# Scores and mix of two self attentions cut into eighths on TensorE, with transposes and projections between the pieces, and ScalarE's copies put in the same order

## The reference, cut to what matters

```python
# stage "sa0"
x = x + _L0_attn_ref(_layernorm(x, axis=-1), ...)
q = rms_norm(proj(Wq), qn_w); k = rms_norm(proj(Wk), kn_w); v = proj(Wv)
attn = jax.nn.softmax(jnp.einsum('bhnd,bhmd->bhnm', q, k) * scale, axis=-1)
out = jnp.einsum('bhnm,bhmd->bhnd', attn, v)       # then @ Wo.T
# stage "sa1": heads go through latents of 32, rotary turning and a causal mask
q_lat = q @ q2l_w.T + q2l_b; k_lat = k @ kv2l_w.T + kv2l_b; v_lat = v @ kv2l_w.T + kv2l_b
q_lat = q_lat * cos + _rotate_half(q_lat) * sin     # k_lat likewise
att = jnp.einsum('bhql,bhkl->bhqk', q_lat @ wqk_w.T + wqk_b, k_lat) * L ** (-0.5)
att = softmax(where(causal, att, -inf)); y = (att @ v_lat) @ l2o_w.T + l2o_b   # then @ cproj_w.T + cproj_b
```

## Time and profile before

| what | value |
|---|---|
| three timed runs | 2615.22, 2619.82, 2624.42 us |
| the profiled execution's own time | 2611.48 us |
| its span in the profile | 2609.7 us |
| mean granted TensorE clock | 0.974 |
| TensorE busy | 2437.4 us, 93% |
| VectorE, GpSimd, ScalarE busy | 65%, 57%, 49% |
| sa0, from its first transposes to its last output product | 1247.1 to 1416.2 us |
| sa1, likewise | 2384.7 to 2582.6 us |

### The profile page before, as it was taken

The page is one execution under the profiler, slowest core; times in us unless marked ns, Lnnn a source line. Parts: engine busy times, 40 slices in busy tenths (PEclk is TensorE's granted clock), DMA queues, the critical chain, the costliest instruction groups (busy, mean ns, idle before and its releaser), DMA issues. The chain is left out here.

```text
span 2609.7 us, 64368 instructions
## 1 busy us (share of the span) xinstructions
PE 2437.4 (93%) x24498; PEld 1899.7 (73%) x24513; DVE 1691.6 (65%) x3969; ACT 1282.5 (49%) x2972; POOL 1475.4 (57%) x1669
## 2 busy tenths in 40 slices
PE   6898999999999999998797999599999999999997
PEld 3456787888878878786565678478888888886565
DVE  5677868686868786874475744466656665653665
ACT  3565656565656565654342333244454445443443
POOL 6896767675757676754672245665456445322233
PEclk9999999999999999999997999799999999999999
DMA  5232211121111111110002459532234224210001
GB/s 166 104 146 84 58 38 48 33 50 35 46 38 42 40 45 36 48 28 14 30 5 85 152 177 303 186 119 77 68 96 103 73 68 97 69 47 15 3 4 35
DMA packets 224820, 190.04 MB, mean 73 GB/s; under 512 B 89218, under 2 KB 212675, under 8 KB 224515
## 3 DMA queue, kind: packets, MB, share of 16 engines
q1 hardware_dynamic: 208994, 153.92, 19.8%
q0 software_dynamic: 9216, 27.28, 4.4%
q10 hardware_dynamic: 6304, 4.72, 0.6%
HBM read 151.53 MB, written 34.31 MB: 71 GB/s over the span
## 5 line engine op out<-in xcount | busy, mean ns | idle before, releaser
L289 POOL TENSOR_TENSOR rk<-ss,neg_half 128x32 f32<-128x32 f32 x64 | 348.7, 5448 | 246.5 <-DVE ss L271 246.5
L1771 PE MATMUL banks<-rowsT,qk 128*128 128x257 f32 x1024 | 243.5, 380 | 0.9 <-ACT qk L1692 0.9
L322 ACT ACTIVATE ksq<-kT 128x512 f32<-128x512 f32 x256 | 161.1, 630 | 160.2 <-DVE kT L265 160.2
L265 DVE COPY kT<-banks 128x512 f32<-128x512 f32 x256 | 176.9, 691 | 61.0 <-PE banks L376 56.9
L376 PE MATMUL banks<-x_hi,wk_hi 128*128 128x256 f32 x1024 | 213.5, 289 | 1.1 <-DVE kT L265 1.0
L1771 PEld LDWEIGHTS banks<-rowsT,qk 128*128 128x128 f32 x1024 | 189.5, 190 | 27.9 <-ACT qk L1692 1.2
L376 PE MATMUL banks<-x_hi,wk_lo 128*128 128x256 f32 x1024 | 206.8, 284 | 0.0
L376 PE MATMUL banks<-x_lo,wk_hi 128*128 128x256 f32 x1024 | 205.6, 282 | 0.3 <-DVE x_lo L257 0.3
L1224 ACT ACTIVATE score<-score,ntop 128x289 f32<-128x289 f32 x256 | 135.4, 530 | 115.5 <-DVE ntop L1104 115.4
L1581 POOL DMA_INDIRECT parts<-scratch_expert,address x128 | 133.6, 1044 | 91.3 <-DVE residual L1477 45.6
L1610 POOL CAST r_hi<-diff 128x512 fp32r<-128x512 f32 x64 | 41.5, 649 | 248.4 <-PE banks L1797 247.6
(11 more groups left out here) (358 smaller groups left out, 6520.2 us busy)
## 6 DMA issues: line engine op xcount, KB each, us to landing
rowsT<-in_ctxT SPq DMA_DIRECT2D x64, 257.0 KB, 2.9
wgu<-in_expert_gu SPq DMA_DIRECT2D x64, 256.0 KB, 3.9
rows<-in_ctx SPq DMA_DIRECT2D x64, 256.0 KB, 3.2
raw<-in_ctx SPq DMA_DIRECT2D x61, 256.0 KB, 2.7
scratch_qT<-qT SPq DMA_DIRECT2D x16, 512.0 KB, 2.7
scratch_kT<-kT SPq DMA_DIRECT2D x16, 512.0 KB, 3.0
q<-scratch_qT SPq DMA_DIRECT2D x64, 128.0 KB
kT<-scratch_kT SPq DMA_DIRECT2D x64, 128.0 KB
```

Of the source, the lines that this page charges most:

```text
L265: nc.vector.tensor_copy(m.kT[:, k, 2 * i:2 * i + 2, 0:ROWS], banks[i % 2].rearrange("p (a r) -> p a r", a=2)).then_inc(s.kT, 1)
L289: nc.gpsimd.tensor_tensor(m.rk[:], m.ss[:], kit.neg_half[:, 0:KF * H], ALU.pow).then_inc(s.rk, 1)
L322: nc.scalar.activation(m.ksq[:, 2 * i:2 * i + 2, :], m.kT[:, k, 2 * i:2 * i + 2, 0:ROWS], ACT.Square).then_inc(s.ksq, 1)
L1771: mm = nc.tensor.matmul(score[h][:, c - h * HALF, 0:CTX], m.qk[:, f, j, c * BT:(c + 1) * BT, :].rearrange("p h q -> p (h q)"), m.rowsT[:, ...
```

## The change

On TensorE the 64 products of the scores are issued in eight parts of 8, those of the mix likewise. In a step the parts of the scores are now mixed with the row transposes (after the first part) and with the transposes of queries and keys in four pairs (after parts five to eight). The parts of the mix are mixed with the latent product (sa1, after the second part), the values (after the fourth) and the groups of the projection (after the fifth, in sa1 also the sixth). The last three parts of the mix in sa0, two in sa1, therefore come behind the projection, right ahead of the next scores. The first part of the scores waits for `shift` of the tile before as well. On ScalarE the copy of the keys comes ahead of the exponentials, and the copy of the mix (`mix_T`) behind the values and `inner`. No product, copy or byte is added or removed.

```diff
@@ ScalarE
                 def step(n, has):
                     if has(2):
                         queries_T(n + 2)
+                    if has(2):
+                        keys_T(n + 2)
                     if has(1):
                         exps(n + 1)
-                    if has(2):
-                        keys_T(n + 2)
                     if has(5):
                         rows_T(n + 5)
-                    if has(0):
-                        mix_T(n)
                     if rotary and has(2):
                         latent_T(n + 2)
                     if has(4):
                         values(n + 4)
                         inner(n + 4)
+                    if has(0):
+                        mix_T(n)
...
@@ TensorE
+                def scores(n, eighth):
+                    if eighth == 0:
...
+                        pe.wait_ge(s.qT, n + 1)
+                        pe.wait_ge(s.kT, n + 1)
+
+                        past(pe, s.shift, n)
+                        past(pe, s.yT, n - 1)
...
+                    c = eighth // 2
+                    for b in (eighth % 2 * 2, eighth % 2 * 2 + 1):
...
+                    if eighth == 7:
+                        mm.then_inc(s.s_ps, 1)
...
                 def step(n, has):
-                    if has(1):
-                        scores(n + 1)
-                    if has(2):
-                        queries_keys_T(n + 2, has(3))
-                    if has(5):
-                        rows_T(n + 5)
+                    for e in range(8):
+                        if has(1):
+                            scores(n + 1, e)
+                        if e == 0 and has(5):
+                            rows_T(n + 5)
+                        if e >= 4 and has(2):
+                            queries_keys_T(n + 2, e - 4, has(3))
                     if has(-1):
                         output(n - 1)
-                    if has(0):
-                        mix(n, has(1))
-                    if rotary and has(2):
-                        latent_T(n + 2)
-                    if has(4):
-                        values(n + 4)
-                        project(n + 4)
+                    for e in range(8):
+                        if has(0):
+                            mix(n, e, has(1))
+                        if rotary and e == 1 and has(2):
+                            latent_T(n + 2)
+                        if e == 3 and has(4):
+                            values(n + 4)
+                        if e in (4, 5) and has(4) and e - 4 < QK // 512:
+                            project(n + 4, e - 4)
```

More of the change, by code:

```diff
@@ L2367, in values @@
                     product(kit.psum(1)[:, D:2 * D], n, slice(QK, QK + D), rotary).then_inc(s.v_ps, 1)
[L2369 to L2380, removed]
@@ L2382, in queries_keys_T, with project @@
-                def queries_keys_T(n, more):
-                    pe.wait_ge(s.qk, n + 1)
-                    if more:
+                def project(n, i):
+                    if i == 0:
+                        pe.wait_ge(s.xlT, n + 1)
+                        past(pe, s.qT, n - 1)
+                        past(pe, s.kT, n - 1)
                         if rotary:
-                            pe.wait_ge(s.lat, n * 2 + 4)
-                            pe.wait_ge(s.cosed, n * 2 + 4)
-                        else:
[L2390 to L2394, removed]
+                            past(pe, s.lat, n * 2)
+                            past(pe, s.cosed, n * 2)
+                        else:
+                            past(pe, s.raw, n)
+                    product(kit.psum(2 + i), n, slice(i * 512, (i + 1) * 512), rotary).then_inc(s.qk_ps, 1)
@@ new lines, in queries_keys_T @@
+                def queries_keys_T(n, part, more):
+                    if part == 0:
+                        pe.wait_ge(s.qk, n + 1)
+                        if more:
+                            if rotary:
+                                pe.wait_ge(s.lat, n * 2 + 4)
+                                pe.wait_ge(s.cosed, n * 2 + 4)
+                            else:
+                                pe.wait_ge(s.raw, n + 2)
+                    i = part // 2
+                    for c in (part % 2 * 2, part % 2 * 2 + 1):
+                        mm = nc.tensor.transpose(kit.psum(2 + i)[:, c * P:(c + 1) * P], m.qk[:, n % 2, (i * HC + c) * BT:(i * HC + c + 1) * BT, :].rearrange("p h l -> p (h l)"), kit.ident[:])
+                    if part % 2 == 1:
+                        mm.then_inc((s.qT_ps, s.kT_ps)[i], 1)
@@ L2398, in latent_T @@
                     nc.tensor.matmul(kit.psum(2), wm.wqk[:], r.qrT[:], start=True, stop=True).then_inc(s.qrT_ps, 1)
[L2400 to L2410, removed]
-                        for a in range(BT):
-                            nc.tensor.matmul(kit.all[:, 4 + a, 0:P], kit.ident16[:], r.causal[:].rearrange("p c k -> p (c k)"), start=True, stop=False, skip_group_check=True)
-                    for c in range(HC):
-                        for b in range(BT):
[L2415 to L2433, removed]
+                def scores(n, eighth):
+                    if eighth == 0:
+                        if n == 0 and extra is not None:
+                            pe.wait_ge(extra.w, 1)
+                        pe.wait_ge(s.qT, n + 1)
+                        pe.wait_ge(s.kT, n + 1)
+                        past(pe, s.shift, n)
+                        past(pe, s.yT, n - 1)
+                        if rotary:
+                            if n == 0:
+                                pe.wait_ge(s.masked, 1)
+                            for a in range(BT):
+                                nc.tensor.matmul(kit.all[:, 4 + a, 0:P], kit.ident16[:], r.causal[:].rearrange("p c k -> p (c k)"), start=True, stop=False, skip_group_check=True)
+                    c = eighth // 2
+                    for b in (eighth % 2 * 2, eighth % 2 * 2 + 1):
+                        for a in range(BT):
+                            rows, tokens = slice(a * S, (a + 1) * S), slice(b * S, (b + 1) * S)
+                            mm = nc.tensor.matmul(score[tokens, a, c, :], m.qT[rows, n % 2, c, tokens], m.kT[rows, n % 2, c, tokens],
+                                                  start=not rotary, stop=True, skip_group_check=True)
+                    if eighth == 7:
+                        mm.then_inc(s.s_ps, 1)
@@ new lines, in mix @@
+                def mix(n, eighth, more):
+                    if eighth == 0:
+                        pe.wait_ge(s.pT, n + 1)
+                        if more:
+                            pe.wait_ge(s.shift, n + 2)
+                    f, i = eighth // 4, eighth // 2 % 2
+                    for a in (eighth % 2 * 2, eighth % 2 * 2 + 1):
+                        for b in range(BT):
+                            rows, part, h = slice(b * S, (b + 1) * S), slice(a * S, (a + 1) * S), f * 2 * BT + 2 * a + i
+                            mm = nc.tensor.matmul(mixed[part, b, f, :], m.v[rows, n % VB, h, :], m.pT[rows, n % 2, place(h), :],
+                                                  start=(i == 0), stop=(i == 1), skip_group_check=True)
+                    if eighth == 7:
+                        mm.then_inc(s.y_ps, 1)
```

## The result

Five runs of the changed kernel took 2686.80 to 2702.74 us, median 2691.49, against 2619.94 before: 1.0281 times as long, 95% interval 1.0263 to 1.0299. It is slower, by 71.5 us where I had forecast some 41, and outside the range. The profiled execution took 2686.8 us, its span is 2685.0 us and the mean granted clock 0.966. Its span is 75.3 us longer than before. Busy times have hardly moved, except TensorE's, which also counts time at the lower clock. The profiled execution is the fastest of the five. The others show a mean granted clock from 0.966 down to 0.957 and spans up to 2700.9 us, so differences of some us between two profiles can be the clock's alone.

A forecast was written before the change was run, and what follows sets the result against it. TensorE, 93% busy, was taken as the bound, with stops for instructions mostly in the mix. 9.5 (sa0) + 25.8 (sa1) + 3.6 - 2.4 + 2.4 + 2.7 = 41.6 us gave a forecast of 2660 us, range 2636 to 2686.

The forecast's parts named there:

- the wait for `yT`: Scores (sa0) or mask product (sa1) wait for the mix's late copy: 1.70 and 2.16 us behind the projection's end.
- the shift wait: Mix waits for VectorE's maximum and subtraction of the scores, no longer covered: some 0.4 us a step, both stages.
- the price of a split: TensorE's way to a large product and back: net 0.11 us, bounds 0 and 0.23; 0.05 in sa1's mix.
- the clock: TensorE's granted clock falls to half behind long gaps: two such cases taken, +2.7 us.
- the tails: Three last steps of each stage, without projection, get the later mix: +2.4 us together, bounds 0 and 4.
- Rivals A: Even instruction stream wins as copies hide behind half-idle ScalarE; steps fall to unstopped length: 2597 us, chance 0.07.
- B (no change): Waits come to half the forecast's, gains and losses cancel: 2620 us within 8, chance 0.06.
- Mix to projection: In sa0, from the mix's start to the projection's end, two splits included: 3.76 us.
- Stops for instructions: TensorE standing for late instruction packets, mostly in the mix: mostly evened out, 0.3 us a sa0 step left, 3.6 us.
- rival D: Split prices at their upper end, 0.23 us each: 23 us more, 2683 us; chance 0.12 together with rival C.
- rival C: Half clock behind every second sa1 gap, every fourth sa0 gap: 12 us, stops +10: 2682; chance 0.12 with rival D.
- the keys' copy: Keys copied ahead of the exponentials save part of a 2.94 us wait at sa0's start: -2.4 us.

The follow-up runs named there:

- e3: Kernel before with only ScalarE's order of the change (keys first, yT behind values and inner) and the wait for shift ahead of the scores: 2690.45 us, 1.0266.
- e5: Changed kernel with yT copied between the square and raw in sa0, between the two lat in sa1: 2657.94 us, 1.0147.
- e9: Kernel before with the keys' copy ahead of the exponentials and the row transposes between the two halves of the scores: 2608.76 us, 0.9968.
- e4: Changed kernel plus three unused products of 256 columns behind the mix's last part in sa1: 2686.31 us, 1.0244.
- e1: Changed kernel with the mix whole again ahead of latent product, values and projection, and yT copied right behind rows_T as before: 2656.89 us, 1.0135.
- e6: Changed kernel with all eight transposes of queries and keys behind the scores, row transposes left in place: 2659.14 us, 1.0163.
- e2: Changed kernel with the scores whole and all transposes, rows included, behind them: 2659.20 us, 1.0149.
- e7: Kernel before with only the keys' copy ahead of the exponentials, and the wait for shift ahead of the scores: 2611.61 us, 0.9977.

## Why the prediction was wrong

The direction, the wait for `yT` and the shift wait hold; the price of a split, the clock and the tails were put too low. Point by point:

- *The wait for yT*: right. Behind the projection 1.60 us against 1.70 predicted in sa0, 1.96 against 2.16 in sa1; e3 and e5 move the loss by that copy's place alone. Rivals A (the copy hides) and B (no change) fall.
- *The shift wait*: right, 0.43 against 0.4.
- *Mix to projection*: near, 3.87 against 3.76.
- *Stops for instructions*: right in kind. The mix's "issue" fell from 19.0 to 3.6 us and the scores' stayed (6.2 before, 6.7 after).
- *The first failed step, the price of a split.* I took 0.11 us; the bounds were 0 and 0.23. A round of small group and pair of transposes takes 0.59 us, where its parts in a stream are 0.15 (8 of 64 products in 1.21) and 0.22. The 8 products take 0.22, which is 0.07 over their share; I had 0.03 there (0.13 for the way out, less 0.10 for queued ones). The pair takes 0.37 to the next small product, so the way back, which I put at 0.08 without a row, costs 0.15. Scores to the last pair: 3.04 against 2.53, so four splits cost 0.24 each rather than 0.11; e9's single split costs 0.22. In the mix they cost less: mix to projection's end takes 0.11 us over my figure in sa0, with two splits at 0.11, and in sa1 7.22 instead of 6.93, with four at 0.05, so some 0.17 and 0.12 each. The value in the scores lies at the upper bound, as rival D had it. Unstopped steps of 10.25 and 14.27 us against 9.67 and 13.61 give 7.0 + 7.9 = 14.9 us too little in the sum, most of it by the splits.
- *The second failed step, "TensorE's clock ... I take two such cases, +2.7"*. In sa1 what lies above twelve unstopped steps is 187.1 - 12 x 14.27 = 15.9 us; in sa0, 127.8 - 12 x 10.25 = 4.8, its stops with it. Together 20.7 where I had 3.6 + 2.7: 14.4 too little. I had one stop of 2.17 us with a fall behind it and one of 1.82 without, and read a threshold between them. Gaps of 1.62 us, one in each of sa1's twelve steps, were followed by the fall in eight of them. e4 (the gap filled: 41 us less of half clock, the stretch 12.6 us shorter) shows that without the gap the falls stay away, and e1 and e5 (none, or a shorter one) agree. e6 and e2 show that the gap isn't the whole of it: the same gap with fewer splits in the scores had 13.7 and 27.3 us of half clock instead of 47.8. What else it takes stays open. This is rival C's mechanism at work. It counted six falls in sa1 and three in sa0; there were eight and one.
- *Elsewhere*: +4.5 us against about 0 for start and tails. The first full step of sa0 starts 2.4 us earlier, which is what I gave the keys' copy; as it is 4.1 us in e7, without the splits, the agreement is in part luck. What lies between the two stretches takes 2.2 us more and what lies behind sa1's 4.7, so the tails lose 6.9 where I had 2.4. One fall of the clock for 6.8 us lies in the last of these (from 2629.65 on); how the rest divides, I have not followed.

14.9 + 14.4 + 4.5 = 33.8 us, which is the miss in the profiled execution (75.3 against 41.6) but for rounding. My own upper ends, 23 us for the splits (D) and 22 for clock and stops (C), cover both failed terms. I treated C and D as alternatives with 0.12 between them, though neither excludes the other, and both did happen.

## What to carry to other kernels

Where small and large products alternate on TensorE, charge each split, there and back, some 0.2 us until a row shows less (0.12 to 0.24 here), and ask what stands behind them that must now wait. Before a copy is put later in its engine's order, look for who waits for the bank it empties: one copy of 0.37 us, started some 4 us later in one stage and some 7 in the other, cost as much here as reordering two engines. A regular gap on TensorE has to be priced twice, once as idle time and once by the granted clock behind it; and a threshold isn't read from two single stops. Two repairs that both bring the clock back don't add up: it comes back once. Rivals that don't exclude each other need a chance for both together.

## What the runs showed of the hardware

- A gap of 1.62 us in each step of sa1 was followed, in eight of twelve steps, by 3.4 or 6.8 us at half clock (0.50, 1.2 GHz), starting 0.7 to 2.3 us after TensorE was busy again. 1.3 us of products in the same place took away 41 of 47.8 us of it (e4). The gain was 12.6 us, three fifths of the 20 that 41 us at half rate could give; in part of such a step TensorE waits for other engines (argued, not shown). With the gap in place, putting the transposes behind the scores took away 34 us of half clock (e6).
- In the scores a split between 32x32 and 128x128 products costs 0.22 to 0.24 us (e9, after), 0.15 of it on the way back to the small ones where a pair of transposes stands between groups of eight.
- The kernel's instruction stops are not removed by thinning only one run: with the mix whole (e1) or the copy moved (e3), stops of up to 2.7 and 2.5 us came back, in e3 most of them in the scores, 19.8 us. Each stop for instructions above 0.25 us, in the kernel before, the changed one and e3, ended 1.2 to 1.6 us after a packet of the instruction queue had ended, and these packets never started closer than 3.3 us to each other.
- What stays open: kernels with the same code for sa0 had 3.4 us of half clock there (after) and 23.9 (e4), and in sa1 the same gap came with 13.7 (e6) to 47.8 us (after). It is the one part of these totals that I can't predict, and it limits what a single profile says to some 7 us a stage.
